# Four chained graph blocks on one core: layer-norm applied on ScalarE, one semaphore per input, and a new order of the steps on every engine

## The chip, the cores and the metric

The kernel runs on one core of a Trainium2 chip. The metric is the device time of one execution in microseconds, as the median of several runs. Profiles show TensorE as PE (its weight loads as PEld), VectorE as DVE, ScalarE as ACT, GpSimd as POOL and SyncE's DMA queue as SPq.

## The reference

There are 32 graphs, each of 256 nodes with 256 features and a dense 256x256 adjacency. Each graph goes through four blocks, and each block ends in a residual sum and a layer norm. In short:

```
x1 = LN(x  + relu([x, (adj @ x) / deg] @ W0.T))
x2 = LN(x1 + gcn3(x1))                 # three layers adj @ (h @ W) + b, relu after the first two
x3 = LN(x2 + (attn @ v) @ W_out + b)   # 8 heads of 64; attn = .33*softmax(q k / 8) + .33*adj + .33*exp(-adj)
x4 = LN(x3 + w * (x3 @ W_v.T))         # w = softmax over nodes of sum_j (q k / 8)_ij adj_ij
LN(x) = (x - mean) / sqrt(var + 1e-5)
```

## The kernel before, in words

Graphs are independent of each other, and one graph's matrices fit on chip. A graph is cut into some fifty steps (a set of transposes, a product, a copy out of PSUM, a softmax part). Each engine has its own list of steps, written out by hand in a function `slot(s)` and repeated for s = -1 to G+4; a step called for a graph outside 0..31 does nothing. The lists name graphs at different distances, so that in one slot the graph steps (blocks 0 and 1) of graph s stand between the attention steps (block 2) of graph s-1 and the tail (block 3) of graph s-2. Engines work through their lists strictly in order; semaphores counted per graph order them against each other.

Products on PE need near-fp32 accuracy. An operand is split into a high part (an fp32r copy made by ACT, function `copy`, L309) and a low part (the difference, made by DVE, function `lo`, L545), and a product is three matmuls (high x high, high x low, low x high; `product`, L911). `HI` and `LO` name the halves of a step that need the high parts alone, and the low part too. Three other shapes run on PE: transposes against the identity (`transpose_tiles`, L925, plain fp32), the attention scores, whose contraction is 64 rows (`scores`, L1118, two heads side by side in row halves of the array, profile form 64\*128), and the attention products `attend` (L1143, two heads in column halves, form 128\*64).

A layer norm is a chain over three engines. DVE makes the sum (`gcn_out` L715, `attention_out` L772, `aggregate` L660 with `relu_residual` L669), then `norm_stats` (L561, two instructions) and `norm_mean` (L582, two). POOL's `norm_rstd` adds epsilon (L291) and raises to -0.5 (L294). DVE's `norm_apply` (L598, two instructions, subtract and multiply) writes x1, x2, x3 or the output, and PE transposes the result.

SyncE loads x, adj and a broadcast mask row of a graph, all counted on one semaphore per buffer parity (`dma_graph`); who needs x waits for all three. At the start the order of the queue is mask, x, adj, mask row of graph 0, then the weights of block 0 and the others.

In PE's list, `scores` of head pair 2 stands after `aggregate`, pair 3 after `hidden(0)`, and pairs 0 and 1 at the slot's end with `x3_transpose` between them; `attend` stands three times (pair 0; pairs 1 and 2; pair 3), the first time directly behind `scores(3)`.

Of the kernel before, what the change touches and what calls it, by code (L numbers as in the profile page):

```python
# [13 lines left out]
def graph_blocks_kernel(nc, x, adj, nodemask, L0_W, L1_W1, L1_b1, L1_W2, L1_b2, L1_W3, L1_b3,  # L14
# [20 lines left out]
    with ctx:  # L35
# [10 lines left out]
        w0_raw = sb("w0_raw", [P, F // P, 2 * F])  # L46
# [82 lines left out]
        rstd = sb("rstd", [P, 4, NT])  # L129

# [3 lines left out]
        XT = 6  # L134
        ADJT = 2
        SUP0 = 1
        SELF = 7
        AGG = 2
        X1T = 0
        GCN = 5  # L140
        X2T = 6
        VALUES = 2
        Y = 2
        X3T = 4
        PROJ3 = 2
        ADJK = 3
        GATE_ROW = 4
        GATE_COL = 3
        SUP = (1, 6, 2)
        HID = (6, 5)  # L150
        QK = (6, 5, 5, 6)
        SCORES = (0, 6, 4, 4)
        PROBT = ((0, 0), (7, 0), (1, 2), (4, 1))
        PV = (3, 7, 0, 1)
        W0T, W3T, MASK = 0, 2, 4
# [7 lines left out]
        def halves(ap):  # L163
# [4 lines left out]
        dma_graph, dma_out = sems("dma_graph"), sems("dma_out")  # L168
        pool_const, pool_ident = sem("pool_const"), sem("pool_ident")
        pool_var, pool_rstd = sems("pool_var", 4), sems("pool_rstd", 4)  # L170

# [19 lines left out]
         dve_gate_prob, dve_x4_pre, dve_y) = (  # L191
# [4 lines left out]
                             "dve_gate_shift", "dve_gate_rsum", "dve_gate_prob", "dve_x4_pre", "dve_y"))  # L196
        dve_sup, dve_hid, dve_x = sems("dve_sup", 3), sems("dve_hid"), sems("dve_x", 3)
# [12 lines left out]
        def live(g):  # L210
            return 0 <= g < G

        def loaded(g):
            return 48 * (g // 2 + 1)
# [9 lines left out]
        FIRST, LAST = -1, G + 5  # L224
# [3 lines left out]
        def _(sp):  # L228
            def load(g):
                b = g % 2  # L230
# [46 lines left out]
        def _(pool):  # L277
            nc.gpsimd.memset(one[:, :], 1.0)
            nc.gpsimd.memset(eps[:, :], LN_EPS)
            nc.gpsimd.memset(minus_half[:, :], -0.5).then_inc(pool_const, 1)  # L280
# [6 lines left out]
            def norm_rstd(k, g):  # L287
                if not live(g):
# [18 lines left out]
        def _(act):  # L307
# [42 lines left out]
            def adj_exp(g):  # L350
                if not live(g):
                    return
                act.wait_ge(dma_graph[g % 2], loaded(g))
# [3 lines left out]
            def mask_bias(g):  # L357
                if not live(g):
                    return
                act.wait_ge(dma_graph[g % 2], loaded(g))  # L360
# [5 lines left out]
                last.then_inc(act_minus_big, 1)  # L366

# [118 lines left out]
            def slot(s):  # L486
                sup_hi(1, s - 3)
                probs_t(s - 4, 2, 0)
                exps(s - 4, 3, 1)
                probs_t(s - 4, 2, 1)  # L490
                hidden(1, s - 3)
                hidden_hi(1, s - 3)
                gate_exps(s - 5)
                out_hi(s - 4, 0)
                out_hi(s - 4, 1)
                out_hi(s - 4, 2)
                sup_hi(2, s - 3)
                probs_t(s - 4, 3, 0)
                probs_t(s - 4, 3, 1)
                x_hi(s - 2)  # L500
                out_hi(s - 4, 3)
                degrees(s - 2)
                x2_hi(s - 3)
                gate_column(s - 5)
                sup0_hi(s - 2)
                qk_hi(s - 3, 0)
                qk_hi(s - 3, 1)
                x3_hi(s - 4)
                exps(s - 3, 0, 0)
                exps(s - 3, 0, 1)  # L510
                tail_qkv(s - 4)
                adj_hi(s - 2)
                qk_hi(s - 3, 2)
                self_copy(s - 2)
                exps(s - 3, 1, 0)
                probs_t(s - 3, 0, 0)
                exps(s - 3, 1, 1)
                probs_t(s - 3, 0, 1)
                qk_hi(s - 3, 3)
                exps(s - 3, 2, 0)  # L520
# [774 lines left out]
```

## Time and profile before

| | |
|---|---|
| median of 3 runs | 1419.85 us (1418.3 to 1422.91) |
| profiled execution: time | 1420.36 us |
| profiled execution: span | 1418.3 us |
| PE busy | 1373.4 us |
| DVE busy | 1232.1 us |
| ACT busy | 921.4 us |
| POOL busy | 131.3 us |
| PE clock granted | 0.987 of full speed over the span |

The span is what the profiler covers, and the execution's own time lies 2.1 us above it. An engine's busy time is the union of its instructions. The end of a matmul is modelled and reaches past the start of the next one, so a short wait of PE does not show as idle; it shows as a larger distance from one start to the next. DVE and ACT instructions overlap in the same way by about 0.1 us, so that what one costs its engine is also read from start to start.

### The profile page before, as it was taken

The numbers are of one execution on the slowest core, as the hardware profiler recorded it, in microseconds if no ns is written. First come the engines' busy times: TensorE is split into PE (matmuls) and PEld (weight loads), VectorE is DVE, ScalarE is ACT, GpSimd is POOL, SyncE is SP. The second block draws the span as 40 slices with busy tenths as digits, with TensorE's granted clock in tenths as the row PEclk, the third lists the DMA queues.
The fourth block names the chain that finished last, engine by engine and source line by source line (L and its number), as shares of the span: only waits on it lengthen the run. The fifth ranks groups of instructions, "written<-read, shape, count | busy, mean of one in ns | idle before, by whom it ended". The sixth has DMA issues, their size and how long they took to land.

```text
span 1418.3 us, 30311 instructions
## 1 busy us (share of the span) xinstructions
PE 1373.4 (97%) x11152; PEld 1218.3 (86%) x11152; DVE 1232.1 (87%) x3821; ACT 921.4 (65%) x2445; POOL 131.3 (9%) x265
## 2 busy tenths in 40 slices
PE   4799999999999999999999999999999999999995
PEld 4788889888889888889888889888888888889884
DVE  4688889889889889889889889889889989889985
ACT  4466766666776666776666776666676666676662
POOL 0000001101001101001101001100001100001100
PEclk8899999999999999999999999999999999999997
DMA  4000000000000000000000000000000000000000
GB/s 146 17 17 17 24 24 2 24 24 25 24 24 4 22 24 25 24 25 9 17 24 24 24 25 11 15 25 24 24 25 20 6 25 24 24 25 9 1 9 22
DMA packets 34050, 32.22 MB, mean 23 GB/s; under 512 B 6896, under 2 KB 33392, under 8 KB 33904
## 3 DMA queue, kind: packets, MB, share of 16 engines
q1 hardware_dynamic: 33904, 30.30, 6.8%
q8 instruction: 89, 1.46, 0.4%
q14 instruction: 57, 0.47, 0.1%
HBM read 21.90 MB, written 8.39 MB: 21 GB/s over the span
## 4 chain that ended last, share of the span: by engine, by line
PE 96%; DVE 1%; ACT 1%; DMA 1%; issue 0%; POOL 0%; SPq 0%; POOLq 0%; DVEq 0%; ACTq 0%
PE psum L911 62%; PE psum L925 14%; PE psum L1143 9%; PE psum L1118 8%; PE psum L1192 1%; PE psum L1195 1%; DMA w_raw<-in_L_gnn_W 1%; PE psum L1205 0%; PE psum L1213 0%; DVE bn L561 0%; ACT wqkv_h L309 0%; POOL rstd L294 0%; DVE x L598 0%; ACT work L444 0%; DVE w_l L545 0%
## 5 line engine op out<-in xcount | busy, mean ns | idle before, releaser
L444 ACT ACTIVATE work<-work,shift 128x256 f32<-128x256 f32 x512 | 254.1, 500 | 16.5 <-DVE shift L738 16.5
L757 DVE SCALAR_TENSOR_TENSOR work<-work,rsum,extra 128x256 f32<-128x256 f32 x512 | 223.2, 478 | 1.4 <-DVE rsum L749 0.2
L738 DVE CUSTOM_DVE_ANT_0 work<-psum,minus_big 128x256 f32<-128x256 f32 x512 | 190.1, 419 | 2.2 <-PE psum L1118 1.6
L309 ACT ACTIVATE work<-psum 128x512 f32<-128x512 f32 x256 | 147.3, 591 | 10.0 <-PE psum L925 9.8
L291 POOL TENSOR_TENSOR mv<-mv,eps 128x2 f32<-128x2 f32 x128 | 34.4, 269 | 1272.8 <-DVE mv L582 1272.8
L911 PE MATMUL psum<-x2T_h,wqkv_h 128*128 128x256 f32 x512 | 149.2, 291 | 1.2 <-DVE x2T_l L545 1.2
L911 PE MATMUL psum<-x2T_l,wqkv_h 128*128 128x256 f32 x512 | 143.3, 280 | 0.0
L911 PE MATMUL psum<-x2T_h,wqkv_l 128*128 128x256 f32 x512 | 143.0, 279 | 0.0
L925 PE MATMUL psum<-ident,work 128*128 128x128 f32 x1024 | 139.8, 274 | 0.1
L1143 PE MATMUL psum<-work,v_sb 128*64 128x256 f32 x1024 | 131.9, 389 | 0.9 <-ACT work L309 0.7
L309 ACT ACTIVATE qkT_h<-psum 128x512 fp32r<-128x512 f32 x128 | 76.6, 599 | 85.7 <-PE psum L911 85.7
L925 PEld LDWEIGHTS psum<-ident,work 128*128 128x128 f32 x1024 | 113.6, 140 | 5.6 <-DVE work L757 0.7
L545 DVE TENSOR_TENSOR sup_l<-psum,sup_h 128x512 fp32r<-128x512 f32 x128 | 88.3, 690 | 29.9 <-ACT sup_h L309 29.9
L911 PE MATMUL psum<-w_h,fT_h 128*128 128x256 f32 x384 | 101.9, 299 | 2.9 <-DVE w_l L545 2.1
L309 ACT ACTIVATE sup_h<-psum 128x512 fp32r<-128x512 f32 x128 | 75.8, 592 | 43.4 <-PE psum L911 43.4
L1143 PEld LDWEIGHTS psum<-work,v_sb 128*64 128x64 f32 x1024 | 64.9, 136 | 41.1 <-issue 12.0
L545 DVE TENSOR_TENSOR qkT_l<-psum,qkT_h 128x512 fp32r<-128x512 f32 x128 | 88.0, 687 | 12.3 <-ACT qkT_h L309 10.0
L911 PEld LDWEIGHTS psum<-x2T_h,wqkv_h 128*128 128x128 f32 x512 | 96.8, 189 | 2.1 <-DVE x2T_l L545 1.5
L444 ACT ACTIVATION_READ_ACCUMULATOR work<-work,shift 128x1 f32 x512 | 97.3, 190 | 0.0
L561 DVE BATCH_NORM_STATS2 bn<-x_pre 128x6 f32<-128x256 f32 x256 | 95.2, 414 | 2.2
L294 POOL TENSOR_TENSOR rstd<-mv,minus_half 128x2 f32<-128x2 f32 x128 | 96.1, 751 | 10.0
L911 PEld LDWEIGHTS psum<-x2T_l,wqkv_h 128*128 128x128 f32 x512 | 96.9, 189 | 0.0
(138 smaller groups left out, 3858.1 us busy)
## 6 DMA issues: line engine op xcount, KB each, us to landing
x_sb<-in_x SPq DMA_DIRECT2D x32, 256.0 KB, 2.8
adj_sb<-in_adj SPq DMA_DIRECT2D x32, 256.0 KB, 3.0
out<-y_sb SPq DMA_DIRECT2D x32, 256.0 KB, 2.1
work<-in_L_gnn_W_qkv SPq DMA_DIRECT2D x1, 1536.0 KB, 9.0
mask_row<-in_nodemask SPq DMA_DIRECT2D x32, 32.0 KB, 3.4
w_raw<-in_L_gnn_W SPq DMA_DIRECT2D x3, 256.0 KB, 6.9
w_raw<-in_L_gnn_W SPq DMA_DIRECT2D x1, 512.0 KB, 8.2
wout_raw<-in_L_gnn_W_out SPq DMA_DIRECT2D x1, 512.0 KB, 9.8
```

Of the source, the lines that this page charges most:

```text
L291: nc.gpsimd.tensor_tensor(mv[:, k, :, 1], mv[:, k, :, 1], eps[:, :], ALU.add) \
L294: nc.gpsimd.tensor_tensor(rstd[:, k], mv[:, k, :, 1], minus_half[:, :], ALU.pow) \
L309: return nc.scalar.activation(dst, src, ACT.Copy, scale=scale)
L444: last = nc.scalar.activation(prob[:, p % 2, i, h], prob[:, p % 2, i, h], ACT.Exp, bias=shift[:, p % 2, h, i:i + 1], scale=-1.0, accum_out ...
L545: return V_.tensor_tensor(dst, src, f32(hi_part), ALU.subtract)
L561: last = V_.bn_stats(out=bn[:, k, t], in_=src[:, t])
L738: last = V_.tensor_tensor_reduce(out=prob[:, p % 2, i, h], in0=bank(SCORES[p] + h)[:, i * N:(i + 1) * N], in1=minus_big[:, g % 2, i], scal ...
L757: last = V_.scalar_tensor_tensor(out=prob[:, p % 2, i, h], in0=prob[:, p % 2, i, h], scalar=rsum[:, p % 2, h, i:i + 1], in1=extra[:, g % 2 ...
L911: last = mm(dst, left, right, start=opens and n == 0, stop=closes and n == len(steps) - 1)
L925: last = nc.tensor.transpose(dst[:, r * N + t * P:r * N + (t + 1) * P], src[:, t, block_of(r)], ident[:, :])
L1118: last = mm(bank(SCORES[p] + h)[:, i * N:(i + 1) * N], qkT[left][rows, p % 2, 0, block_of(i)], qkT[right][rows, p % 2, 1], start=n == 0 an ...
L1143: last = mm(bank(PV[p])[h * D:(h + 1) * D, 0:N], v_sb[:, k, (2 * p + h) * D:(2 * p + h + 1) * D], probT[:, p % 2, h, k], start=k == 0, sto ...
```

## The change

- `norm_apply` moves from DVE to ACT. It becomes an `Identity` activation with a scale and a bias per row, so POOL makes a third result: it negates the mean after adding epsilon, and after the power multiplies the two (`minus_mean`).
- x, adj and the mask row get semaphores of their own. At the start the queue carries x, then block 0's weights, then adj and the mask row.
- All five lists are reordered and the PSUM banks reassigned; waits that guard a bank's reuse are removed and added accordingly. In PE's list, `scores` of pairs 0 and 1 stand together, and so do `attend` of pairs 0 and 1.

```diff
@@ PSUM banks @@
+        XT, ADJT, SUP0, SELF, AGG, X1T, GCN, X2T = 2, 6, 7, 5, 5, 3, 2, 3
...
@@ sync @@
-            load(0)
+            load_x(0)
             sp.dma_start(w0_raw[:, :, :], L0_W.rearrange("(n p) f -> p n f", p=P)).then_inc(dma_w0, 16)
+            load_rest(0)
@@ gpsimd: norm_rstd @@
                 nc.gpsimd.tensor_tensor(mv[:, k, :, 1], mv[:, k, :, 1], eps[:, :], ALU.add) \
                     .then_inc(pool_var[k], 1)
+                nc.gpsimd.tensor_tensor(minus_mean[:, k], mv[:, k, :, 0], minus_one[:, :], ALU.mult) \
+                    .then_inc(pool_mean[k], 1)
                 pool.wait_ge(pool_var[k], once(g))
                 nc.gpsimd.tensor_tensor(rstd[:, k], mv[:, k, :, 1], minus_half[:, :], ALU.pow) \
+                    .then_inc(pool_pow[k], 1)
+                pool.wait_ge(pool_pow[k], once(g))
+                pool.wait_ge(pool_mean[k], once(g))
+                nc.gpsimd.tensor_tensor(minus_mean[:, k], minus_mean[:, k], rstd[:, k], ALU.mult) \
                     .then_inc(pool_rstd[k], 1)
@@ scalar: norm_apply, in place of DVE's @@
+                act.wait_ge(pool_rstd[k], once(g))
...
+                for t in range(NT):
+                    last = nc.scalar.activation(dst[:, t], src[:, t], ACT.Identity, bias=minus_mean[:, k, t:t + 1],
+                                                scale=rstd[:, k, t:t + 1])
+                last.then_inc(act_y if k == 3 else act_x[k], 1)
@@ tensor @@
             def x_transpose(g):
-                pe.wait_ge(dma_graph[g % 2], loaded(g))
+                pe.wait_ge(dma_x[g % 2], loaded(g))
...
             def qk(g, p):
+                if p == 2:
+                    pe.wait_ge(dve_scores, nth2(g, p - 1, 1))
...
             def probs_t(g, p, h):
                 if p == 0 and h == 1:
-                    pe.wait_ge(act_probT, nth2(g, p, 0))
+                    pe.wait_ge(act_v, once(g))
...
```

The new lists of the three engines that do most of the work, each a `slot(s)` in whole. First PE:

```diff
+    hidden(0, s - 1, LO)
+    attend(s - 2, 0)
+    attend(s - 2, 1)
+    support(1, s - 1, HI)
+    support(1, s - 1, LO)
+    probs_t(s - 2, 2, 0)
+    gate_row(s - 3)
+    probs_t(s - 2, 2, 1)
+    x_transpose(s)
+    hidden(1, s - 1, HI)
+    hidden(1, s - 1, LO)
+    probs_t(s - 2, 3, 0)
+    probs_t(s - 2, 3, 1)
+    attend(s - 2, 2)
+    support(2, s - 1, HI)
+    support(2, s - 1, LO)
+    attend(s - 2, 3)
+    gcn_out(s - 1, HI)
+    gcn_out(s - 1, LO)
+    support0(s, HI)
+    project_out(s - 2, HI)
+    project_out(s - 2, LO)
+    support0(s, LO)
+    adj_transpose(s)
+    x2_transpose(s - 1)
+    gate_column(s - 3)
+    self_product(s)
+    qk(s - 1, 0)
+    x3_transpose(s - 2)
+    qk(s - 1, 1)
+    tail_project(s - 2, HI)
     tail_project(s - 2, LO)
+    scores(s - 1, 0)
+    scores(s - 1, 1)
     tail_adj_k(s - 2)
+    values(s - 1, HI)
     aggregate(s, HI)
     aggregate(s, LO)
+    values(s - 1, LO)
+    qk(s - 1, 2)
+    qk(s - 1, 3)
+    probs_t(s - 1, 0, 0)
+    probs_t(s - 1, 0, 1)
     scores(s - 1, 2)
     x1_transpose(s)
+    scores(s - 1, 3)
     support(0, s, HI)
     support(0, s, LO)
     probs_t(s - 1, 1, 0)
     probs_t(s - 1, 1, 1)
     hidden(0, s, HI)
```

DVE:

```diff
+    attention_out(s - 4)
+    norm_stats(2, s - 4)
+    norm_mean(2, s - 4)
+    x2_lo(s - 3)
+    tail_out(s - 5)
+    adj_extra(s - 3)
+    sup0_lo(s - 2)
+    x2_bias(s - 3)
+    norm_stats(3, s - 5)
+    x3_lo(s - 4)
+    qk_lo(s - 3, 0)
+    qk_lo(s - 3, 1)
+    tail_k(s - 4)
+    scores(s - 3, 0, 0)
+    scores(s - 3, 0, 1)
+    norm_mean(3, s - 5)
+    scores(s - 3, 1, 0)
+    adj_lo(s - 2)
+    scores(s - 3, 1, 1)
+    tail_gate(s - 4)
+    recip_sums(s - 3, 0)
+    probs(s - 3, 0, 0)
+    aggregate(s - 2)
+    relu_residual(s - 2)
+    norm_stats(0, s - 2)
+    norm_mean(0, s - 2)
+    recip_sums(s - 3, 1)
+    probs(s - 3, 0, 1)
+    qk_lo(s - 3, 2)
+    probs(s - 3, 1, 0)
+    qk_lo(s - 3, 3)
+    scores(s - 3, 2, 0)
+    probs(s - 3, 1, 1)
+    x1_lo(s - 2)
+    x1_bias(s - 2)
+    scores(s - 3, 2, 1)
+    sup_lo(0, s - 2)
+    degrees(s - 1)
+    scores(s - 3, 3, 0)
+    scores(s - 3, 3, 1)
+    recip_sums(s - 3, 2)
+    probs(s - 3, 2, 0)
+    hidden_lo(0, s - 2)
+    probs(s - 3, 2, 1)
+    recip_sums(s - 3, 3)
+    probs(s - 3, 3, 0)
+    sup_lo(1, s - 2)
+    probs(s - 3, 3, 1)
+    adj_sum(s - 2)
+    out_lo(s - 3, 0)
+    gate_maximum(s - 4)
+    hidden_lo(1, s - 2)
+    out_lo(s - 3, 1)
+    x_lo(s - 1)
+    sup_lo(2, s - 2)
+    out_lo(s - 3, 2)
+    out_lo(s - 3, 3)
+    gcn_out(s - 2)
+    norm_stats(1, s - 2)
+    norm_mean(1, s - 2)
+    gate_probs(s - 4)
```

ACT:

```diff
+    hidden(0, s - 5)
+    hidden_hi(0, s - 5)
+    exps(s - 6, 3, 0)
+    exps(s - 6, 3, 1)
+    sup_hi(1, s - 5)
+    probs_t(s - 6, 2, 0)
+    out_hi(s - 6, 0)
+    probs_t(s - 6, 2, 1)
+    x_hi(s - 4)
+    hidden(1, s - 5)
+    out_hi(s - 6, 1)
+    hidden_hi(1, s - 5)
+    probs_t(s - 6, 3, 0)
+    probs_t(s - 6, 3, 1)
+    mask_bias(s - 5)
+    out_hi(s - 6, 2)
+    sup_hi(2, s - 5)
+    out_hi(s - 6, 3)
+    gate_exps(s - 7)
+    norm_apply(3, s - 8)
+    norm_apply(1, s - 5)
+    sup0_hi(s - 4)
+    x2_hi(s - 5)
+    gate_column(s - 7)
+    self_copy(s - 4)
+    norm_apply(2, s - 6)
+    qk_hi(s - 5, 0)
+    x3_hi(s - 6)
+    qk_hi(s - 5, 1)
+    tail_qkv(s - 6)
+    adj_hi(s - 4)
+    exps(s - 5, 0, 0)
+    exps(s - 5, 0, 1)
+    exps(s - 5, 1, 0)
+    exps(s - 5, 1, 1)
+    degrees(s - 3)
+    values(s - 5)
+    qk_hi(s - 5, 2)
+    qk_hi(s - 5, 3)
+    probs_t(s - 5, 0, 0)
+    norm_apply(0, s - 4)
+    probs_t(s - 5, 0, 1)
+    adj_exp(s - 4)
+    x1_hi(s - 4)
+    exps(s - 5, 2, 0)
+    sup_hi(0, s - 4)
+    probs_t(s - 5, 1, 0)
+    exps(s - 5, 2, 1)
+    probs_t(s - 5, 1, 1)
```

## Rows read from the trace of the kernel before

**Rows 1.** Page, part 1: busy us, share of the span, instructions.

```profile
PE 1373.4 (97%) x11152; PEld 1218.3 (86%) x11152; DVE 1232.1 (87%) x3821; ACT 921.4 (65%) x2445; POOL 131.3 (9%) x265
```

**Rows 2.** Chain that ended last, in order of time (start us, us, what): slots' first long piece.

```profile
69.14 3.28 PE psum L911 x20
...
1340.00 3.28 PE psum L911 x20
```

**Rows 3.** Timeline of PE (start us, us, engine line op, tiles): scores and transposes.

```profile
735.46 0.65 PE L925 MATMUL psum<-ident,x 128*128 128x128 f32 x4
736.04 0.51 PE L1118 MATMUL psum<-qkT_h 64*128 64x256 f32 x4
736.38 0.40 PE L1118 MATMUL psum<-qkT_l,qkT_h 64*128 64x256 f32 x4
736.62 0.40 PE L1118 MATMUL psum<-qkT_h,qkT_l 64*128 64x256 f32 x4
736.95 0.45 PE L911 MATMUL psum<-w_h,x3T_h 128*128 128x384 f32 x1
...
739.17 0.28 PE L911 MATMUL psum<-x2T_h,wqkv_h 128*128 128x256 f32 x1
...
740.53 0.60 PE L925 MATMUL psum<-ident,adj_sb 128*128 128x128 f32 x4
740.89 0.31 PE L1192 MATMUL psum<-k,adjT_h 128*128 128x128 f32 x1
```

**Rows 4.** Timeline of PE: eight transposes before a product that waits for `sup_h`.

```profile
758.62 1.03 PE L925 MATMUL psum<-ident,work 128*128 128x128 f32 x8
759.58 0.39 PE L911 MATMUL psum<-adjT_h,sup_h 128*128 128x256 f32 x1
```

**Rows 5.** Timeline of POOL: epsilon and power of norms 3 and 0.

```profile
744.20 0.34 POOL L291 TENSOR_TENSOR mv<-mv,eps 128x2 f32<-128x2 f32 x1 [10.65 <-DVE mv L582]
744.62 0.81 POOL L294 TENSOR_TENSOR rstd<-mv,minus_half 128x2 f32<-128x2 f32 x1
748.06 0.20 POOL L291 TENSOR_TENSOR mv<-mv,eps 128x2 f32<-128x2 f32 x1 [2.63 <-DVE mv L582]
748.33 0.69 POOL L294 TENSOR_TENSOR rstd<-mv,minus_half 128x2 f32<-128x2 f32 x1
```

**Rows 6.** Page, part 5: ACT's activation with a per-row bias.

```profile
L444 ACT ACTIVATE work<-work,shift 128x256 f32<-128x256 f32 x512 | 254.1, 500 | 16.5 <-DVE shift L738 16.5
```

**Rows 7.** Timeline of ACT: the copy of the tail's projection.

```profile
739.37 0.81 ACT L309 ACTIVATE qkv<-psum 128x768 f32<-128x768 f32 x1
```

**Rows 8.** Timeline of DVE: softmax, tail and norm steps back to back.

```profile
738.76 0.42 DVE L738 CUSTOM_DVE_ANT_0 work<-psum,minus_big 128x256 f32<-128x256 f32 x1
...
739.54 0.72 DVE L561 BATCH_NORM_STATS2 bn<-x_pre 128x6 f32<-128x256 f32 x2
740.22 0.23 DVE L785 CAST k<-qkv 128x128 fp32r<-128x128 f32 x1
...
740.69 0.88 DVE L757 SCALAR_TENSOR_TENSOR work<-work,rsum,extra 128x256 f32<-128x256 f32 x2
...
743.28 0.68 DVE L545 TENSOR_TENSOR qkT_l<-psum,qkT_h 128x512 fp32r<-128x512 f32 x1
743.88 0.24 DVE L582 BATCH_NORM_AGGREGATE mv<-bn 128x2 f32<-128x6 f32 x2
744.04 0.85 DVE L757 SCALAR_TENSOR_TENSOR work<-work,rsum,extra 128x256 f32<-128x256 f32 x2
...
745.31 0.88 DVE L660 SCALAR_TENSOR_TENSOR x_pre<-psum,rdeg,self_part 128x256 f32<-128x256 f32 x2
...
746.94 0.75 DVE L561 BATCH_NORM_STATS2 bn<-x_pre 128x6 f32<-128x256 f32 x2
747.73 0.25 DVE L582 BATCH_NORM_AGGREGATE mv<-bn 128x2 f32<-128x6 f32 x2
```

**Rows 9.** Chain that ended last, first stretch: block 0's weights.

```profile
2.66 8.20 DMA w_raw<-in_L_gnn_W
```

More of the change, by code:

```diff
@@ L129, in graph_blocks_kernel @@
         rstd = sb("rstd", [P, 4, NT])
+        minus_mean = sb("minus_mean", [P, 4, NT])
+        minus_one = sb("minus_one", [P, NT])
         psum = ctx.enter_context(nc.psum_tensor("psum", [P, 8, 512], F32))
[L134 to L155, printed above, removed]
+        XT = 2
+        ADJT = 6
+        SUP0 = 7
+        SELF = 5
+        AGG = 5
+        X1T = 3
+        GCN = 2
+        X2T = 3
+        VALUES = 0
+        Y = 5
+        X3T = 3
+        PROJ3 = 0
+        ADJK = 7
+        GATE_ROW = 0
+        GATE_COL = 4
+        SUP = (6, 7, 3)
+        HID = (7, 3)
+        QK = (4, 2, 2, 6)
+        SCORES = (4, 2, 4, 0)
+        PROBT = ((7, 0), (2, 3), (1, 5), (1, 5))
+        PV = (6, 4, 7, 4)
+        W0T, W3T, MASK = 0, 4, 3
         def bank(n):
@@ L501, in slot @@
[L501 to L516, printed above, removed]
@@ L827, in slot @@
             def slot(s):
-                scores(s - 2, 0, 0)
-                x3_lo(s - 3)
-                scores(s - 2, 0, 1)
-                scores(s - 2, 1, 0)
-                scores(s - 2, 1, 1)
-                recip_sums(s - 2, 0)
-                norm_stats(3, s - 4)
-                tail_k(s - 3)
-                probs(s - 2, 0, 0)
-                adj_lo(s - 1)
-                qk_lo(s - 2, 2)
-                norm_mean(3, s - 4)
-                probs(s - 2, 0, 1)
-                tail_gate(s - 3)
@@ L842, in slot @@
-                aggregate(s - 1)
-                relu_residual(s - 1)
-                norm_stats(0, s - 1)
-                norm_mean(0, s - 1)
-                scores(s - 2, 2, 0)
-                recip_sums(s - 2, 1)
-                norm_apply(0, s - 1)
-                scores(s - 2, 2, 1)
-                probs(s - 2, 1, 0)
-                x1_lo(s - 1)
-                probs(s - 2, 1, 1)
-                qk_lo(s - 2, 3)
-                sup_lo(0, s - 1)
-                recip_sums(s - 2, 2)
@@ L1235, in slot @@
                 hidden(0, s, HI)
-                hidden(0, s, LO)
-                scores(s - 1, 3)
-                attend(s - 1, 0)
-                support(1, s, HI)
-                support(1, s, LO)
-                probs_t(s - 1, 2, 0)
-                probs_t(s - 1, 2, 1)
-                hidden(1, s, HI)
-                hidden(1, s, LO)
-                gate_row(s - 2)
-                attend(s - 1, 1)
-                attend(s - 1, 2)
-                support(2, s, HI)
-                support(2, s, LO)
-                probs_t(s - 1, 3, 0)
-                probs_t(s - 1, 3, 1)
-                gcn_out(s, HI)
-                gcn_out(s, LO)
-                x_transpose(s + 1)
-                attend(s - 1, 3)
-                project_out(s - 1, HI)
-                project_out(s - 1, LO)
-                x2_transpose(s)
-                support0(s + 1, HI)
-                support0(s + 1, LO)
-                gate_column(s - 2)
-                qk(s, 0)
-                qk(s, 1)
-                scores(s, 0)
-                x3_transpose(s - 1)
-                scores(s, 1)
-                tail_project(s - 1, HI)
             pe.wait_ge(pool_ident, 2)
```

190 lines of the change are left out of this document (56 added, 134 removed).

## The prediction

> **What bounds the kernel now.** I read the page's busy times first: PE is busy 97% of the span, DVE 87%, ACT 65% [rows 1]. So PE's list sets the end, and only what shortens PE's list, or makes PE wait, counts. The chain of waits, in order of time, says how regular this is: a piece of the tail's projection comes back 30 times between 69.14 and 1340.00 [rows 2], so one slot takes 1270.86 / 30 = 42.36 us, and 30 slots hold nine tenths of the span. Everything below is a sum per slot, times 30, and a small one for the two ends.
>
> PE's busy share hides what happens inside a slot, so the third view is its timeline, read from start to start. Twelve 384-column matmuls take 2.22 us (736.95 to 739.17) and twelve 256-column ones 1.36 (739.17 to 740.53) [rows 3]: I take 0.46 ns per column, 0.118 us for 256 columns. Four transposes take 0.36 before an ordinary matmul (740.53 to 740.89) [rows 3], and each further one 0.11 (1.03 us for eight in rows 4 against 0.60 for four in rows 3).
>
> **A change of array shape costs about 0.19 us.** Four score matmuls go in 0.24 us, but the first four of a block take 0.34 and the last four 0.33; the four transposes between two score blocks take 0.58 where 0.36 is normal [rows 3]. So about 0.1 is lost in the block left and 0.1 in the block entered, at each change between full, row-halved and column-halved shape. TensorEngine Tiling (Array Packing) in the Trainium skill (Key Properties) says that changing the mode drains the engine; these rows agree, and give it its price here.
>
> **The change on PE.** Before, a slot visits the row-halved shape four times and the column-halved one three times; `scores(3)` and `attend(0)` touch, so there are 13 changes. After, it visits each three times and none touch: 12. That is -0.2 us; the products themselves are the same.
> Second, PE waits in places already. Eight transposes before the product that needs `sup_h` take 0.96 [rows 4] where 0.36 + 4 x 0.11 = 0.80 would do: 0.16 of waiting. The same form occurs twice more per slot; I bound those between nothing and 0.16 and take 0.06 each. After, 14 transposes stand before `hidden(1)`, and `attend(3)` before `gcn_out`, so only the one before `hidden(0)` is left: -0.2 us (0.16 to 0.3).
> With nothing else a slot would be 42.36 - 0.4 = 42.0.
>
> **The change on DVE and ACT.** DVE loses eight `norm_apply` instructions per graph, some 3 us of a slot (an estimate: the two statistics instructions of the same size take 0.75 [rows 8]), and ACT gains eight. Neither is the bound, so the lighter DVE gives nothing by itself. What matters is how long each norm's chain gets, and what PE has to do meanwhile.
> POOL: from the end of `norm_mean` to the end of the power takes 1.04 us in norm 0 (747.73 + 0.25 to 748.33 + 0.69) and 1.31 in norm 3 (743.88 + 0.24 to 744.62 + 0.81) [rows 5, 8]. The two new multiplies show nowhere; the nearest row is the epsilon addition, the same form, 0.20 or 0.34. One stands between addition and power, where some 0.08 of it is hidden in the wait (+0.12 or +0.26), one after the power with a wait of 0.08 (+0.28 or +0.42). POOL's part becomes 1.44 to 1.99.
> ACT: the nearest row to the new activation is the exponential with a per-row bias, 0.50 us [rows 6]; two overlap to 0.90, and 0.05 each for the hand-over in and out: 1.0. Its bounds are 0.7 (a plain copy) and 1.1.
> Each chain's DVE part, when DVE is free: 0.2 to start, 0.72 for the sum (a 512-element operation with its wait, 745.31 to 746.94 holds it and the 0.91 before), 0.79 for the statistics, 0.25 for the mean [rows 8]: 1.96.
>
> *x3* (norm 2). Chain: 1.96 + 1.44 = 3.4 on POOL's fast side; but ACT's list has `self_copy` ahead, which ends near 3.84; then 1.0: 4.8 (4.9 on the slow side). PE's cover behind `project_out`: 28 matmuls of 256 columns (`support0` LO, `self_product`, `qk(0)`) 3.3, eight transposes 0.87, `gate_column` with its shape changes 0.4: 4.57. PE waits 0.25 (0.2 to 0.35).
> *x2* (norm 1). Chain 4.4 to 4.95; cover `support0` and `project_out`, 36 matmuls 4.25, and `adj_transpose` 0.43: 4.7. Wait 0 (to 0.3).
> *x1* (norm 0). Here DVE is late. I count from the end of `tail_project`. The copy of the projection ends at 0.1 + 0.05 + 0.81 [rows 7]: 0.96. DVE's new list puts `tail_k` first, in order, so the softmax's first pass of pairs 0 and 1 waits behind it. Then, back to back [rows 8]: `tail_k` 0.47 (740.22 to 740.69); four `scores` steps, 0.78 with a reciprocal, 0.69 without, 2.76; `norm_mean` 0.16; `adj_lo` 0.60; reciprocal, `probs` and `tail_gate` 1.27 + 0.2; `aggregate` and `relu_residual` 1.63; statistics and mean 1.04. Together 8.13, so norm 0's mean is out at 9.1. POOL: 10.5 or 11.1. ACT is copying `probs_t(0, 0)` until 10.8; then 0.95: x1 is there at 11.75 or 12.05. PE's cover: 24 score matmuls 1.63; `tail_adj_k` 1.0 with the change; `values`, `aggregate`, `qk(2)`, `qk(3)`, 12 x 512 and 36 x 256 columns x 0.46 ns = 7.07; eight transposes 0.96; `scores(2)` 0.91: 11.57. PE waits 0.2 to 0.5; I take 0.35, the middle, since both POOL speeds occur.
> What is queued behind: behind x1 wait its transposes, then `scores(3)`, which also needs ACT's `probs_t(0, 1)`, itself behind the new activation (ready by then). By the same walk the steps from `support(0)` round to `gcn_out` have 0.1 to 0.3 us in hand at each hand-over, so nothing more is added there.
>
> GpSimd shares SBUF interfaces with VectorE and contends with DVE instructions that have two SBUF inputs, says GPSIMD Engine Reference in the Trainium skill (Key points). The slow POOL rows do stand beside such an instruction (744.04, `work` by `extra`), the fast ones beside one that reads PSUM. In the new list `probs(0, 1)` follows norm 0's mean, so by that rule its wait would be the 0.5.
>
> **Sum.** Per slot -0.4 + 0.25 + 0 + 0.35 = +0.2: 42.56, and 30 slots give +6 us. At the ends: block 0's weights land at 2.66 + 8.20 = 10.86 [rows 9] and hold up the first product; moved ahead of adj and the mask row they land sooner, by between 1 and 3.5, I take 2.5, as ACT's `degrees(0)` now stands before `x_hi(0)` and waits for adj. x2 of graph 0 gets `support0(1)` and `adj_transpose(1)` as cover, 1.2 net. Against that, three chains without cover get 0.65 longer (2), and x2 of graph 31 has only `project_out` before it, 1.5. Together 0. So 1420.36 + 6 = 1426.4 in the profiled execution, and since that lay 0.5 above the median, 1426 for the median. About 0.3%, 4.3 us, is what a measurement of this kernel can tell from no change.
>
> **The rivals.**
> A, the waits are not there: the order was made so that x1 and x3 come in time. That takes 0.3 us of error in two covers of 4.6 and 11.6 us, which I can't exclude: ACT's activation may cost a copy's 0.3 (chain 0.2 shorter), and `probs_t` may come earlier. Then only the -0.4 counts: 30 x -0.4 = -12, with the start 1408. For it: my walks go by starts that are good to 0.05 each. Chance 0.3.
> B, slower by more: POOL's slow side everywhere, norm 1 too, and first transposes after a wait that start from a drained array (0.05 each). x1 0.5, x3 0.35, x2 0.3, 0.1 more: +0.85 per slot, 30 x 0.85 = 25 us, 1440 or, with half of it, 1433. It decides from the point where norm 1's chain exceeds 4.7 us. Against it: norm 1 has no such DVE instruction beside it. Chance 0.15.
> C, no net change: x1 waits for ACT, not POOL, 0.2, and x3 0.2; +0.0 per slot, 1420. Chance 0.2.
> The change does what it says for DVE in all of them; that DVE's relief shortens the slot is the one thing that rows 1 exclude.
> My forecast, x1 and x3 wait together about 0.6, 1423 to 1432, has 0.35.
>
> **How the numbers follow.** 1426 is the likeliest case's. The range runs from A to B's half, 1406 to 1436, its own from 1423 to 1432. Faster by over 0.3% (below 1415.6): A, 0.3. Within 0.3% (to 1424.1): C and the lower edge of mine, 0.24. Slower: 0.46.
>
> **What would show it.** Right: a slot of 42.4 to 42.8; waits of weight loads for `x1` and `x3` from ACT in nearly every slot, near 0.35 and 0.25; DVE idle before `tail_k` for over 1 us; the four transposes between scores 0 and 1 gone; block 0's weights landed before 9.9 us instead of 10.86. POOL's multiplies 0.2 or 0.34. Wrong: a slot below 42.2 with no waits at those transposes, or a new long wait elsewhere (a `probs_t` waiting for DVE, `qk` for x2's low part), which my walk has in hand by 0.1 only.

## The result, and the profile after

| | before | after |
|---|---|---|
| median of 4 runs each | 1421.38 us (1418.3 to 1423.34) | 1437.87 us (1436.44 to 1440.62) |
| ratio to before, 95% interval | | 1.012, 1.0094 to 1.0146 |
| profiled execution: time, span | 1420.36 us, 1418.3 us | 1440.62 us, 1438.8 us |
| one slot | 42.36 us [rows 2] | 42.93 us |

The change makes the kernel 1.2% slower. The forecast was slower too, by 0.3 to 0.5%, and its range ended at 1436, 2 us short of the median.

The page of the kernel after: busy time of each engine, and the chain that ended last by engine.

```profile
PE 1368.3 (95%) x11152; PEld 1219.5 (85%) x11152; DVE 1152.3 (80%) x3565; ACT 1031.7 (72%) x2701; POOL 176.9 (12%) x522
...
PE 87%; ACT 9%; DVE 1%; issue 1%; DMA 0%; POOL 0%; SPq 0%; ACTq 0%; POOLq 0%; DVEq 0%
...
L397 ACT ACTIVATE x<-x_pre,minus_mean,rstd 128x256 f32<-128x256 f32 x192 | 104.5, 592 | 111.6 <-POOL minus_mean L313 109.9
```

Beside [rows 1]: DVE fell from 87% to 80%, ACT rose from 65% to 72%, as the move says. PE is still the engine that sets the end, but it fell from 97% to 95%: it waits more. The last line is the new activation (L397, `norm_apply`): 592 ns each, where the prediction took 0.50 us from the exponential of [rows 6].

The chain of waits of the kernel after, in order of time (start us, us, what): the same piece of a slot at its first, second and last appearance.

```profile
105.67 7.16 PE psum L933 x48
148.59 7.17 PE psum L933 x48
...
1350.54 7.17 PE psum L933 x48
```

(1350.54 - 105.67) / 29 = 42.93 us per slot, 0.57 more than [rows 2]. Times 30 that is 17 us, and the medians differ by 16.5: the loss is in the slot. The two profiled executions are 20.3 us apart; most of the 3 us beyond the slots lie at the end, where the `tail_project` steps of the last two graphs start 32.52 us apart (1388.00 and 1420.52) and before started 29.64 apart (1371.99 and 1401.63).

The table of waits of the kernel after (who waits for whom: us in total, times, longest).

```profile
DVE k L810 <- ACT qkv L328: 55.1, 32, 4.4
...
PEld psum L947 <- ACT x L397: 51.6, 65, 6.3
...
PE psum L947 <- ACT x L397: 38.6, 65, 6.0
```

L947 is a transpose on PE. The 65 waits for `x` from ACT are two in nearly every slot, x3's and x1's; both stand in the timelines. First x3, on PE, ACT and POOL (start us, us, engine, line, op, tiles, [idle before]).

```profile
651.70 0.28 PE L933 MATMUL psum<-wout_h,oT_l 128*128 128x256 f32 x1
651.81 0.62 PE L933 MATMUL psum<-w_h,fT_l 128*128 128x256 f32 x4
...
656.18 0.28 PE L933 MATMUL psum<-x2T_h,wqkv_l 128*128 128x256 f32 x1
656.76 0.66 PE L947 MATMUL psum<-ident,x 128*128 128x128 f32 x4 [0.30 <-ACT x L397]
```

```profile
655.14 0.60 ACT L328 ACTIVATE self_part<-psum 128x512 f32<-128x512 f32 x1 [1.14 <-PE psum L933]
655.63 1.08 ACT L397 ACTIVATE x<-x_pre,minus_mean,rstd 128x256 f32<-128x256 f32 x2
```

```profile
653.85 0.20 POOL L304 TENSOR_TENSOR mv<-mv,eps 128x2 f32<-128x2 f32 x1 [2.50 <-DVE mv L619]
654.00 0.20 POOL L306 TENSOR_TENSOR minus_mean<-mv,minus_one 128x2 f32<-128x2 f32 x1
654.15 0.69 POOL L309 TENSOR_TENSOR rstd<-mv,minus_half 128x2 f32<-128x2 f32 x1
654.92 0.20 POOL L313 TENSOR_TENSOR minus_mean<-minus_mean,rstd 128x2 f32<-128x2 f32 x1
```

The last product of `qk(0)` starts at 656.18 and would be followed at 656.30, one product of 0.118 later; the transposes start at 656.76. The wait is 0.46 us (the idle time in brackets, 0.30, is what remains of it behind the modelled end of the product). POOL is done at 655.12, but ACT's two activations start at 655.63, behind `self_copy`, and end at 656.71.

Then x1.

```profile
672.12 0.40 PE L1135 MATMUL psum<-qkT_h,qkT_l 64*128 64x256 f32 x4
673.01 0.66 PE L947 MATMUL psum<-ident,x 128*128 128x128 f32 x4 [0.49 <-ACT x L397]
...
674.18 0.40 PE L1135 MATMUL psum<-qkT_h,qkT_l 64*128 64x256 f32 x4
674.50 0.39 PE L933 MATMUL psum<-w_h,fT_h 128*128 128x256 f32 x1
```

```profile
671.27 0.59 ACT L328 ACTIVATE work<-psum 128x512 f32<-128x512 f32 x1
671.87 1.09 ACT L397 ACTIVATE x<-x_pre,minus_mean,rstd 128x256 f32<-128x256 f32 x2
```

```profile
670.03 0.41 POOL L304 TENSOR_TENSOR mv<-mv,eps 128x2 f32<-128x2 f32 x1 [14.92 <-DVE mv L619]
670.40 0.44 POOL L306 TENSOR_TENSOR minus_mean<-mv,minus_one 128x2 f32<-128x2 f32 x1
670.80 0.68 POOL L309 TENSOR_TENSOR rstd<-mv,minus_half 128x2 f32<-128x2 f32 x1
671.56 0.27 POOL L313 TENSOR_TENSOR minus_mean<-minus_mean,rstd 128x2 f32<-128x2 f32 x1
```

```profile
669.71 0.25 DVE L619 BATCH_NORM_AGGREGATE mv<-bn 128x2 f32<-128x6 f32 x2
...
669.93 0.85 DVE L782 SCALAR_TENSOR_TENSOR work<-work,rsum,extra 128x256 f32<-128x256 f32 x2
...
671.30 0.87 DVE L782 SCALAR_TENSOR_TENSOR work<-work,rsum,extra 128x256 f32<-128x256 f32 x2
```

The last four matmuls of `scores(3)` hand over in 0.32 us (674.18 to 674.50); those of `scores(2)` take 0.89, so x1's wait is 0.57. Two things end together before it: POOL at 671.83, and on ACT the copy of `probs_t(0, 0)` at 671.86. Then come 1.09 us of activations. Of the two POOL is the one that holds them, by 0.13 us: behind a copy alone they start before the copy has ended, 0.47 us after its start (C below), and here 0.60.

0.46 + 0.57 = 1.03 of waiting; without it the slot would be 41.90. The saving of 0.46 that this leaves against 42.36 has the size that the prediction gave to the new order, 0.4; how it divides between the changes of shape and the waits that went was not measured.

### The profile page after: what moved, and what is told of

Read it like the earlier page. It is cut to its first block, busy times and chain, and to the rows that moved or that the text cites. A ratio compares the mean times of both kernels' runs of the same rounds, so it can differ in the third digit from the quotient of the medians.

```text
span 1438.8 us, 30697 instructions
## 1 busy us (share of the span) xinstructions
PE 1368.3 (95%) x11152; PEld 1219.5 (85%) x11152; DVE 1152.3 (80%) x3565; ACT 1031.7 (72%) x2701; POOL 176.9 (12%) x522
## 4 chain that ended last, share of the span: by engine, by line
PE 87%; ACT 9%; DVE 1%; issue 1%; DMA 0%; POOL 0%; SPq 0%; ACTq 0%; POOLq 0%; DVEq 0%
PE psum L933 58%; PE psum L947 12%; PE psum L1160 8%; PE psum L1135 6%; ACT x L397 5%; PE psum L1208 1%; ACT qkT_h L328 1%; ACT work L328 1%; PE psum L1211 1%; ACT self_part L328 1%; PE psum L1220 0%; DMA wv_raw<-in_L_gnn_W_v 0%; PE psum L1228 0%; ACT work L477 0%; DVE bn L598 0%
## 5 line engine op out<-in xcount | busy, mean ns | idle before, releaser
L782 DVE SCALAR_TENSOR_TENSOR work<-work,rsum,extra 128x256 f32<-128x256 f32 x512 | 223.6, 479 | 3.6 <-issue 0.2
L304 POOL TENSOR_TENSOR mv<-mv,eps 128x2 f32<-128x2 f32 x128 | 38.6, 301 | 1247.4 <-DVE mv L619 1247.4
L397 ACT ACTIVATE x<-x_pre,minus_mean,rstd 128x256 f32<-128x256 f32 x192 | 104.5, 592 | 111.6 <-POOL minus_mean L313 109.9
L933 PE MATMUL psum<-x2T_h,wqkv_h 128*128 128x256 f32 x512 | 145.9, 285 | 1.4 <-DVE x2T_l L582 1.2
L947 PE MATMUL psum<-ident,work 128*128 128x128 f32 x1024 | 138.5, 273 | 0.9 <-DVE work L782 0.6
L947 PEld LDWEIGHTS psum<-ident,work 128*128 128x128 f32 x1024 | 115.4, 141 | 3.3 <-DVE work L782 2.4
L947 PE MATMUL psum<-ident,x 128*128 128x128 f32 x384 | 62.2, 285 | 38.6 <-ACT x L397 38.6
```

The costliest lines, as they stand in the source:

```text
L304: nc.gpsimd.tensor_tensor(mv[:, k, :, 1], mv[:, k, :, 1], eps[:, :], ALU.add) \
L397: last = nc.scalar.activation(dst[:, t], src[:, t], ACT.Identity, bias=minus_mean[:, k, t:t + 1], scale=rstd[:, k, t:t + 1])
L782: last = V_.scalar_tensor_tensor(out=prob[:, p % 2, i, h], in0=prob[:, p % 2, i, h], scalar=rsum[:, p % 2, h, i:i + 1], in1=extra[:, g % 2 ...
L933: last = mm(dst, left, right, start=opens and n == 0, stop=closes and n == len(steps) - 1)
L947: last = nc.tensor.transpose(dst[:, r * N + t * P:r * N + (t + 1) * P], src[:, t, block_of(r)], ident[:, :])
```

## The experiments

The slot is measured in each as above, over 29 slots of the chain of waits, so it is that of the profiled execution; the medians are over all runs. "Before", run beside them, had medians of 1418.2 to 1420.5. Ratios are to it, with their 95% intervals. Line numbers shift by a few between kernels.

| edit | median us (runs) | ratio | slot us |
|---|---|---|---|
| the change | 1437.87 (4) | 1.012 | 42.93 |
| A `self_copy` behind x3's norm | 1437.55 (4) | 1.0134 [1.0107, 1.0161] | 42.86 |
| B activation with bias alone | 1427.54 (1) | | 42.55 |
| C POOL's multiplies left out | 1433.42 (1) | | 42.81 |
| D all norms on DVE, new order | 1415.31 (10) | 0.9973 [0.9956, 0.9991] | 42.26 |
| E A, and x3 in two buffers | 1425.16 (10) | 1.0038 [1.0021, 1.0054] | 42.45 |
| F norms 0 and 2 on DVE, other loads | 1413.2 (6) | 0.996 [0.9939, 0.998] | 42.04 |
| G norms on ACT, order of before | 1499.73 (1) | | 44.89 |
| H D, and `hidden_lo(0)` earlier | 1411.22 (4) | 0.9942 [0.992, 0.9965] | 42.06 |
| I E, and norm 0 on DVE | 1416.55 (10) | 0.9986 [0.9975, 0.9997] | 42.15 |
| J H, attention products apart | 1440.23 (4) | 1.0166 [1.0149, 1.0183] | 43.07 |
| K one semaphore, loads in old order | 1440.47 (1) | | 42.92 |
| L I, and `hidden_lo(0)` earlier | 1410.96 (6) | 0.9942 [0.9927, 0.9958] | 41.96 |

The theory was that the whole loss is the two waits, and that each is the length of a chain that ends in ACT's activations. The rivals: a fuller ACT costs something by itself; the new order on PE saves nothing, or the waits would be there without the move.

**A. What stands ahead of x3 on ACT.**

```diff
-                self_copy(s - 4)
                 norm_apply(2, s - 6)
+                self_copy(s - 4)
```

> The changed kernel with one exchange in ACT's list: norm 2's activations stand before self_copy. Theory (PE waits for x3 because ACT does self_copy first and then two activations of 0.59 us): POOL is done 0.5 us before ACT starts on x3, so x3 comes 0.5 earlier and PE's wait at its transposes, 0.46 to 0.52 per slot, goes: slot 42.92 - 0.5 = 42.4, the whole 15 us faster than the changed kernel, near 1422. Rival (the new order itself is too tight, and something else is late next, DVE first): the slot stays within 0.1 of 42.92.

The timelines of ACT and DVE in A:

```profile
652.20 1.09 ACT L397 ACTIVATE x<-x_pre,minus_mean,rstd 128x256 f32<-128x256 f32 x2 [1.55 <-DVE x_pre L848]
```

```profile
651.24 0.87 DVE L848 SCALAR_TENSOR_TENSOR x_pre<-qkv,gate_col,x 128x256 f32<-128x256 f32 x2
```

The same DVE step in the kernel after:

```profile
654.58 0.87 DVE L848 SCALAR_TENSOR_TENSOR x_pre<-qkv,gate_col,x 128x256 f32<-128x256 f32 x2
```

Almost nothing came of it, 0.07 us per slot: the theory's 42.4 missed, and the rival's slot, within 0.1 of 42.92, came true. With `self_copy` out of the way ACT still sits idle, for 1.55 us, until DVE's `tail_out` (L848) ends at 652.11. `tail_out` reads the x3 of the graph before, and x3 has one buffer: the wait `reuse(act, dve_x4_pre, ...)`, which was on DVE before and cost nothing there because `tail_out` stands on the same engine, now crosses from DVE to ACT. In the kernel after, `tail_out` ends at 655.45, so with the same 0.09 of hand-over ACT could have started at 655.54 in place of 655.63. The two causes end 0.09 us apart, which is why A gained 0.07; the prediction's walk has no such wait, and the table of waits lists it once in 32 graphs.

**E. The same with x3 in two buffers** (`x3[:, g % 2]`, the reuse wait one graph later).

> The exchange of the last run kept (norm 2's activations before self_copy), and x3 in two buffers, so that the activation no longer waits for tail_out of the graph before, which reads x3. In the last run's trace ACT stood idle 1.55 us for exactly that DVE step and started on x3 when it ended. Theory (x3 is held by two things at the same moment, self_copy on ACT and the one x3 buffer through tail_out on DVE, so freeing one gives nothing): ACT starts when POOL is done, 0.4 to 0.45 earlier, PE's wait for x3 goes to 0.1 or less, slot 42.86 - 0.45 = 42.4, near 1421. Rival (something else is late for x3 too, or PE's own order makes the 0.5): slot 42.8 or more.

The slot fell by another 0.41 to 42.45, the waits for `x` from ACT from 64 to 35, and the median by 12.4 us. In its timeline the transposes of x3 follow the product before them by 0.12 us, so that wait is gone. The slot is as expected (42.4), the median 4 us above the 1421 expected: the ten runs spread from 1421.37, the profiled one, to 1427.44. So x3's wait had two causes that end within 0.09 us of each other, and only taking away both freed it.

**B. The activation's own price.** The reciprocal root is left out (`scale=` dropped), so x is only shifted by the mean.

```diff
-  nc.scalar.activation(..., ACT.Identity, bias=minus_mean[:, k, t:t + 1], scale=rstd[:, k, t:t + 1])
+  nc.scalar.activation(..., ACT.Identity, bias=minus_mean[:, k, t:t + 1])
```

> The changed kernel with the norm's activation given a per-row bias alone; the multiplication by 1/sqrt(var) is left out. Theory (an activation with two per-row operands is dearer than the row with one, 0.59 against 0.50, and that is what the forecast's sum missed): the activation takes 0.50 and two 0.90 in place of 1.09, PE's waits for x1 and x3 each shrink by 0.19, slot 42.92 - 0.38 = 42.54, the forecast's 42.56. Rival (the price is contention with DVE or POOL for SBUF): still 0.59, slot 42.92.

Its group on the page of B:

```profile
L397 ACT ACTIVATE x<-x_pre,minus_mean 128x256 f32<-128x256 f32 x192 | 86.9, 501 | 117.1 <-POOL minus_mean L313 115.4
```

With one operand per row the activation takes 501 ns, the 0.50 of [rows 6]; with two, 592. Two of them stand in each wait, so 0.18 each; the slot fell by 0.38, two waits of 0.19.

**C. POOL's multiplies.** Both are left out, and the mean itself is given as bias.

> The changed kernel without POOL's two multiplies per norm; the mean itself is given as bias, so its sign and its product with 1/sqrt(var) are left out. Theory (ACT is busy with other steps until 655.63 for x3 and 671.8 for x1, so POOL is hardly the one that is late): POOL's chain becomes 0.5 to 0.7 shorter, but x1 comes only 0.1 earlier and x3 not at all, slot 42.8. Rival (POOL's multiplies are what lengthens the chains): both waits shrink by 0.5, slot 41.9 to 42.0.

ACT's timeline at x1:

```profile
668.36 0.59 ACT L322 ACTIVATE work<-psum 128x512 f32<-128x512 f32 x1
668.83 1.09 ACT L391 ACTIVATE x<-x_pre,mv,rstd 128x256 f32<-128x256 f32 x2
```

The slot fell by 0.12, all of it from x1: the activations now start 0.47 us after the copy's start and not 0.60. Behind the multiplies the next thing is ready at once: the copy of `probs_t(0, 0)` at x1, `self_copy` and `tail_out` at x3.

**D and H. The new order alone**, all norms back on DVE (each `norm_apply` at a place that I chose in DVE's list, `qk_lo(3)`, `x1_lo` and `x1_bias` exchanged with their neighbours, two multiplies fewer on POOL; the exchanges are in F, H, I, J and L too); in H also the low part of `hidden(0)` ahead of `probs(2, 0)` on DVE.

> The changed kernel with that part undone: all four norms applied on DVE again (two instructions each, POOL without multiplies), in the new order of steps; DVE's list gets the four steps, and around x1 qk_lo(3), x1_lo and x1_bias change places with their neighbours. Theory (the order is sound and worth 0.5 per slot, the move to ACT is what costs): no wait at x1 or x3, slot 41.9 (41.8 to 42.1), near 1407, faster than both. Rival (DVE with 3 us more per slot is late elsewhere, the order needs its relief): a slot of 42.9 or more, with weight loads waiting for DVE.

> The run with all four norms on DVE in the new order, with one exchange: hidden_lo(0) ahead of probs(2, 0) in DVE's list. Theory (what kept that run at 42.23 and not 41.9 is the hidden layer's low part coming 0.25 late, behind probs(2, 0)): slot 41.98, the whole 7 us below that run, 1407 to 1409. Rival (DVE is just full there and the wait moves on to probs_t): slot 42.2.

D has neither of the two waits to speak of, and one new one inside `support(1)`, for `hidT_l` from DVE; so it missed the 41.9 and 1407 that were expected. H removes that wait and takes 0.20 off the slot, to 42.06 and 1411 where 41.98 and 1407 to 1409 were expected. So the new order is worth 5 us by itself and 7 with H's exchange, each against "before" run beside it, and in this order the move of the norms to ACT costs 1437.87 - 1415.31 = 22.6 us.

**G. The move alone**, in the order and with the banks of before.

> One part of the change alone: the kernel before, in its own order and banks, with the norms applied on ACT (two activations, POOL's two multiplies), each placed beside the high-part copy that follows it. Theory (each chain gets 0.9 to 1.1 us longer: 0.4 to 0.8 on POOL, 0.35 for the dearer activations; x1 had no time in hand before, x3 0.3, x2 0.7): PE waits about 0.9 for x1, 0.3 for x2, 0.5 or more at x3 or at scores(1) behind a later qk copy; slot 42.36 + 1.7 = 44.1, 1470 (1455 to 1480). Rival (the move itself is harmless, it is the new order that waits): slot within 0.3 of 42.36.

I expected 1470. The table of waits of G:

```profile
PEld psum L938 <- ACT x L388: 61.5, 65, 6.3
...
PEld psum L924 <- ACT sup_h L319: 36.6, 34, 1.1
PE psum L924 <- ACT sup_h L319: 28.6, 32, 0.9
```

The slot is 44.89, 2.5 more than before. The waits for x were foreseen, the third is new: `sup_h`, nearly 1 us in every slot. ACT's timeline in G, between two copies for `hidden(0)` and `support(1)`:

```profile
616.29 0.63 ACT L319 ACTIVATE hidT_h<-hid 128x512 fp32r<-128x512 f32 x1
616.83 1.08 ACT L388 ACTIVATE y_sb<-x_pre,minus_mean,rstd 128x256 f32<-128x256 f32 x2
617.81 0.89 ACT L374 ACTIVATE minus_big<-mask_row,big_col 128x256 f32<-128x256 uint8 x2
618.61 0.57 ACT L319 ACTIVATE work<-psum 128x512 f32<-128x512 f32 x1
...
620.07 0.58 ACT L319 ACTIVATE sup_h<-psum 128x512 fp32r<-128x512 f32 x1
```

ACT runs without a gap, and norm 3 (`y_sb`), which nobody waits for, takes 1.1 us in front of an operand that PE needs. So the move had a second price in the old order, which the new one avoids. How much of G comes from where I put norm 3, and how much from the order, was not separated.

**F. Two norms on each engine**, `hidden_lo(0)` earlier, and the gate's weights loaded ahead of adj.

> A version meant to be fast: the new order, norms 0 and 2 (those with a tight deadline) on DVE, norms 1 and 3 on ACT, hidden_lo(0) ahead of probs(2, 0) in DVE's list, and the block-3 weights loaded before adj of graph 0. Theory: of the waits left with all norms on DVE (0.25 for the hidden layer's low part, 0.1 at x3, 0.08 at sup_h) the first goes, slot 42.23 - 0.3 = 41.95, and the first products start 3 us earlier: 1404 (1400 to 1408), against 1420 before. Rival (PE's list can't go under 42.2 because matmuls themselves pace it): slot 42.2, 1413 to 1415.

The slot is as in H, and the total 9 us above what I expected. The load order gained nothing; the slots' first piece comes at 105.06 against 103.13 in H, 1.9 us later. The expectation had counted a gain at the start that isn't there (see K).

**I and L. Three norms on ACT, norm 0 on DVE**, x3 in two buffers; L with `hidden_lo(0)` earlier as well.

> The changed kernel with x3 in two buffers and the norms of x2, x3 and the output on ScalarE as in the run before (slot 42.46 us there, with one wait left, 0.55 us before x1's transposes), and norm 0 alone given back to VectorE. If the waits for x1 and x3 are all that the changed kernel lost, the slot is 41.9 to 42.0 us and the median 1408 to 1411 us, with three of the four norms still on ScalarE. If a norm on ScalarE costs the slot something by itself (a fuller engine, later operands for others), the slot stays above 42.2 us and the median at 1416 or more.

> The kernel of the run before last in this call's series (norm 0 on VectorE, the other three on ScalarE, x3 in two buffers, slot 42.15 us, median 1416.55), with the low part of hidden(0) moved ahead of probs(2, 0) on VectorE, which removes the 0.24 us wait inside support(1). The slot is then 41.9 us and the median 1416.5 - 30 x 0.24 = 1409.5 us, a little under the kernel with all norms on VectorE (slot 42.03, median 1411), so that three norms on ScalarE cost nothing. By the rival, that ScalarE's norms cost the slot something as soon as nothing else holds it, the wait comes back elsewhere and the median stays at 1414 or more.

I missed its interval on the high side (42.15), and its median, 1416.55, is what the rival gave; the expectation had forgotten the `hidT_l` wait that D had shown; it is in I's table of waits (30 times), and only L decides. L, without that wait, has the shortest slot of all. The same piece in L's chain of waits, at 104.30 and 29 slots later:

```profile
104.30 7.14 PE psum L952 x48
...
1320.99 7.16 PE psum L952 x48
```

(1320.99 - 104.30) / 29 = 41.96, what the prediction gave for a slot without new waits (42.0), with 192 of the 256 activations still on ACT. The rival that a fuller ACT costs something by itself falls: only the waits did. L and H are 0.6% faster than the kernel before and 1.9% faster than the kernel after, and can't be told from each other.

**J. What a change of array shape costs.** H with one step moved on PE:

```diff
                 attend(s - 2, 0)
-                attend(s - 2, 1)
                 support(1, s - 1, HI)
+                attend(s - 2, 1)
                 support(1, s - 1, LO)
```

> The kernel with all norms on VectorE and the new order (slot 42.03 us, median 1411), with one step moved on PE alone: attention product 1 stands between the two halves of support(1) and no longer beside attention product 0. That adds two changes of array shape per slot and no work. By the prediction's 0.19 us for a change the slot is 42.41 us, the median 1422 to 1423. If putting two products together saves nothing, and the slot is short for another reason (waits that went), it stays at 42.03 to 42.1 us and 1411.

Timeline of PE in J, then the same place in H:

```profile
676.12 1.08 PE L1179 MATMUL psum<-work,v_sb 128*64 128x256 f32 x8
677.83 0.38 PE L952 MATMUL psum<-w_h,hidT_h 128*128 128x256 f32 x1 [0.62 <-ACT hidT_h L333]
...
678.95 1.08 PE L1179 MATMUL psum<-work,v_sb 128*64 128x256 f32 x8
679.97 0.74 PE L952 MATMUL psum<-w_h,hidT_l 128*128 128x256 f32 x4
```

```profile
622.11 1.95 PE L1179 MATMUL psum<-work,v_sb 128*64 128x256 f32 x16
623.99 0.38 PE L952 MATMUL psum<-w_h,hidT_h 128*128 128x256 f32 x1
```

The slot grew by 1.01 us, far more than the 0.38 expected. The first attention product takes 1.71 to its successor and the second 1.02: 0.69 is a wait for `hidT_h`, which the two products side by side had covered. What is left, 1.01 - 0.69 = 0.32, is two changes of shape, 0.16 each. So putting pairs together is worth two things, the changes and a longer cover, and the second was the larger here.

**K. The inputs' semaphores and the load order**, both as before, the rest as changed.

> The changed kernel with one semaphore for the three inputs of a graph, and the first loads in the old order (x, adj, mask row, then block 0's weights). In the slot nothing waits for an input, so it stays 42.92 us. The prediction counts the load order as 2.5 us at the start: the first product then starts 2.5 us later than in the changed kernel. By the trace of the changed kernel, where the start hangs on a later load (the gate's value weights, landing after 10 us), it moves by under 1 us.

The load that the start of the kernel after hangs on in its chain of waits; then the timelines of PE at the first product, and the windows table (stretch, its length, busy us of PE, PEld, DVE, ACT, POOL, granted clock, DMA share, GB/s), each for the kernel after and then for K:

```profile
3.65 6.92 DMA wv_raw<-in_L_gnn_W_v
```

```profile
14.18 0.58 PE L933 MATMUL psum<-w_h,fT_h 128*128 128x256 f32 x1 [2.02 <-DVE w_l L582]
```

```profile
38.00:42.00 4.00, 2.26 (x11) 1.99 (x11) 2.26 (x5) 1.47 (x3) 0.00 (x0) 0.50 0.02 4
```

```profile
16.12 0.39 PE L934 MATMUL psum<-w_h,fT_h 128*128 128x256 f32 x1 [2.33 <-DVE w_l L583]
```

```profile
38.00:42.00 4.00, 2.25 (x19) 2.08 (x19) 3.48 (x8) 1.60 (x4) 0.00 (x0) 1.00 0.00 0
```

The load order does bring the first product forward by 1.94 us, less than the prediction's 2.5 and more than the 1 us that was expected of K. Block 0's weights land 5.5 us sooner than before, but then the start hangs on `wv_raw`, which lands at 10.57. But the slots' first piece starts at 105.67 in the kernel after and at 105.63 in K: nothing of it is left. In between, PE works in pieces with long waits while the pipeline fills, and the granted clock drops to 0.50, the 1.2 GHz level, in both (24 to 36 us in K). In the kernel after it is still there from 38 to 42 us, where K has 1.00: the twelve products that start at 40.49 in the one take 2.90 us, and those that start at 40.68 in K take 1.67. Why the clock came back later in the one than in the other wasn't tried. The separate semaphores and the load order together are worth nothing that this one run could show.

## Why the prediction was right or wrong

**Right.** The bound (PE's list) and the form of the loss: a sum per slot, made of two waits, for x3 and x1 from ACT, none for x2, and about nothing at the ends (the medians differ by 16.5 where 30 slots make 17; the profiled executions leave 3 us for the ends). The slot without new waits: 42.0 predicted, 41.90 by the timeline and 41.96 in L. The price of a change of shape: 0.19 predicted, 0.16 in J. DVE's lighter load gave nothing. The walk to x1: the mean of norm 0 was to be out 9.1 us after `tail_project`; the row above ends at 669.96, and the scores behind `tail_project` start at 660.88, 9.08 later. PE's cover was to be 11.57; it is 672.44 - 660.88 = 11.56. DVE waits before `tail_k` for 55.1 / 32 = 1.7 us, block 0's weights had landed by 1.65 + 3.7 = 5.35 instead of 10.86 us (sooner by 5.5, where 1 to 3.5 was given).

**Wrong: the size of the two waits.** They were put at 0.25 + 0.35 = 0.60 and are 0.46 + 0.57 = 1.03. That is 0.43 x 30 = 13 us; less some 2 us for a slightly larger saving it is 11 of the miss of 11.9. By the steps of the working:
- *x1, 0.22 too little: the activations.* "The nearest row to the new activation is the exponential with a per-row bias, 0.50 us." That row has one operand per row, the new instruction two, and takes 0.592. From the end of the copy ahead of it (671.86) to the transposes (673.01) it is 1.15 us, where the term was 0.95: 0.20 of the 0.22. This is the step that failed. B confirms the price from the other side: at 0.50 the slot is 0.38 shorter, the forecast's 42.55, and its one run, 1427.54, is 10.3 us below the change's median and 1.5 above the forecast.
- *x1: POOL.* "I take 0.35, the middle, since both POOL speeds occur." For norm 0 only the slow one does: 1.87 us from the end of the mean (669.96) to 671.83, where the middle of 1.44 to 1.99 is 1.7. It cost the sum just 0.03: the forecast's two cases free the activations at 10.8 and 11.1, in the middle 10.95, and here POOL is done at 10.95 and the copy of `probs_t(0, 0)` at 10.98. The copy alone would have held them nearly as long; C, where this POOL chain is 0.49 shorter (667.04 to 668.42) for 0.12 us of slot, says so. GPSIMD Engine Reference in the Trainium skill (Key points) says that GpSimd contends with DVE instructions that have two SBUF inputs. The rows agree, and show what sets the size: the addition and the first multiply beside L782 end 0.51 and 0.91 us after its pair of instructions starts (669.93), the last multiply 0.53 after the next pair (671.30), and x3's last multiply 0.54 after the pair of L848, which has two SBUF inputs as well. Each ends just behind one of the pair's instructions of some 0.43 us, so they took 0.41, 0.44, 0.27 and 0.20 by where in one they began. The 0.5 that the prediction worked out by that rule was nearer to the 0.57, but not by its reason: its POOL was done at 11.1, and the missing part was the activations.
- *x3, 0.21 too little: three small ones.* Counted from the end of `project_out` at 651.81, `self_copy` ends at 3.93 where 3.84 was forecast (0.09), the cover is 4.49 where it was 4.57 (0.08), and the activations with their hand-over take 1.02 from there, where 1.0 was taken: the dearer instruction was made up for by its overlap with `self_copy`, which the prediction didn't count. The rest is rounding (4.84 - 4.57 is 0.27).
- *x3: a wait left out.* "But ACT's list has `self_copy` ahead": the prediction listed what stands ahead on ACT and not the semaphore that the moved step takes along. A and E show it. It made no part of the miss, since it ends 0.09 before `self_copy`, but whoever had acted on the prediction would have moved `self_copy` alone and gained 0.07, where both changes gain 0.07 + 0.41 = 0.48.

**Wrong without effect.** The start: of the 2.5 us for the loads 1.9 show at the first product, 0 at the first full slot (K). By the medians the sum of 0 for both ends held; by the profiled executions the ends cost 3 us, which were put at nothing, most of it in the last two graphs.

**The rivals and the range.** A (no waits) had 0.3, on the ground that 0.3 us of error would do; the waits are three times that. B (slower by more) is what the size came nearest to, 0.57 per slot of its 0.85, but not by its mechanism: norm 1 never waited, and POOL was slow in norm 0's chain and in norm 3's first addition, not in those of x2 and x3. Its sum was wrong as well: 25 us on 1420 are 1445, not 1440. C (no change) was out by the same 0.4 as the forecast and more. The upper bounds of the two waits, 0.35 and 0.5, give 42.36 - 0.4 + 0.85 = 42.81 and 13.5 us, 1433, which is also half of B; the range ended at 1436. But the 0.5 held POOL's slow side and not the activation's own upper bound of 1.1 on top, which was written down with the term itself and would have added 0.1 to each wait, 6 us: 1439. The bound of an unknown price belongs in every term that holds it.

## What to carry to other kernels

A step that is moved to another engine takes its waits along: one that was free because both ends stood on one engine becomes a handover between two, and a single buffer can hold it. Of an operation that the trace does not show, count the operands: a row with one per-row operand was a lower bound for one with two, and a price that stands in several waits brings its error in each. Relieving an engine that isn't the bound gains nothing by itself, and the move is paid for in latency where the bound engine waits for the moved step; here norms 1 to 3 could be moved at no cost, with a second buffer for x3, and norm 0, at its place in this list, could not.

## What the runs showed of the hardware

- ACT's activation of 128x256 fp32 takes 0.50 us with a bias per row and 0.59 with a bias and a scale per row (B against the change).
- POOL's addition and multiplication on 128x2 take 0.20 us in x3's chain. Beside a DVE instruction with two inputs in SBUF they took 0.41 and 0.44 where they began near its start, and 0.27 and 0.20 where they began late in it; the power took 0.68 and 0.69 in the two chains shown.
- Two more changes between the full and the column-halved shape cost 0.32 us beyond the wait that came with them, 0.16 each (J).
- A first product that starts 1.9 us sooner was worth nothing at the first full slot; from 38 to 42 us that kernel had a granted clock of 0.50 and the other 1.00 (K). That the clock is the reason is not shown.
